# Storing the last of four images in two halves: two PSUM banks, two additions, two stores

## What is computed

```python
def _L3_conv_ref(x, w_qkv, w_out, b_out):
    xf = x.reshape(b, c, n)                          # n = h * w = 256
    qkv = jnp.einsum('oc,bcn->bon', w_qkv, xf)
    qkv = qkv.reshape(b, 3, HEADS, DIM_HEAD, n)
    q, k, v = (qkv[:, 0], qkv[:, 1], qkv[:, 2])
    k = jax.nn.softmax(k, axis=-1)
    context = jnp.einsum('bhdn,bhen->bhde', k, v)
    out = jnp.einsum('bhde,bhdn->bhen', context, q)
    out = out.reshape(b, HEADS * DIM_HEAD, n)
    out = jnp.einsum('oc,bcn->bon', w_out, out) + b_out[None, :, None]
    return out.reshape(b, -1, h, w)
...
x = x + _L3_conv_ref(_gn(x), L3_conv_w_qkv, L3_conv_w_out, L3_conv_b_out)
return x
```

## Time and profile before

| what | us |
|---|---|
| median of 3 timed executions | 65.83 |
| lowest, highest of them | 65.51, 68.95 |
| the profiled execution, its own time | 65.53 |
| its span in the profile | 63.7 |
| granted TensorE clock, mean over the span | 1.0 of full speed |

### The profile page before, as it was taken

The page is one execution under the profiler, slowest core; times in us unless marked ns, Lnnn a source line. Parts: engine busy times, 40 slices in busy tenths (PEclk is TensorE's granted clock), DMA queues, the critical chain, the costliest instruction groups (busy, mean ns, idle before and its releaser), DMA issues. The chain is left out here.

```text
span 63.7 us, 1376 instructions
## 1 busy us (share of the span) xinstructions
PE 58.2 (91%) x362; PEld 47.8 (75%) x362; DVE 48.1 (76%) x218; ACT 36.9 (58%) x113; POOL 34.1 (53%) x98
## 2 busy tenths in 40 slices
PE   2999999999999699799999999999999799999920
PEld 2778748898999488388888688887876579899800
DVE  3848998539899999825579999999999786546350
ACT  5206527997997791780025897537075876796600
POOL 5864986878996364250058997976852142000000
PEclk9999999999999999999999999999999999999999
DMA  0797000000000000000000000000000000001133
GB/s 0 218 241 284 12 0 0 0 0 0 15 5 0 0 0 0 0 5 0 10 0 0 0 0 0 5 0 0 0 0 0 0 0 0 0 10 43 39 116 131
DMA packets 1432, 1.81 MB, mean 28 GB/s; under 512 B 145, under 2 KB 1169, under 8 KB 1425
## 3 DMA queue, kind: packets, MB, share of 16 engines
q1 hardware_dynamic: 1424, 1.73, 8.7%
HBM read 1.20 MB, written 0.52 MB: 27 GB/s over the span
## 5 line engine op out<-in xcount | busy, mean ns | idle before, releaser
L1621 PE MATMUL bank<-x,dw_diag 128*128 128x256 f32 x44 | 11.1, 390 | 0.1
L358 POOL TENSOR_TENSOR gn_rstd<-gn_var_eps,minus_half 128x1 f32<-128x1 f32 x12 | 6.6, 550 | 6.7 <-DVE gn_var_eps L846 6.4
L1621 PEld LDWEIGHTS bank<-x,dw_diag 128*128 128x128 f32 x44 | 7.9, 190 | 1.2 <-DVE x L1115 0.3
L1450 PE MATMUL bank<-warm 128*128 128x256 bf16 x46 | 6.9, 314 | 1.2 <-POOL warm L341 1.2
L1450 PEld LDWEIGHTS bank<-warm 128*128 128x128 bf16 x46 | 5.1, 113 | 2.3 <-POOL warm L341 1.1
L1579 PE MATMUL bank<-vt,probT 128*128 128x128 f32 x32 | 5.1, 281 | 0.0
L1550 PE MATMUL bank<-t,q 128*128 128x256 f32 x16 | 5.0, 392 | 0.0
L679 ACT ACTIVATE h<-dw_sum,kept_scale_bias 128x256 f32<-128x256 f32 x4 | 2.4, 598 | 4.1 <-DVE kept_scale_bias L1182 4.1
L1592 PE MATMUL bank<-signs,conv_blocks 128*128 128x256 bf16 x36 | 4.3, 276 | 0.4 <-ACT signs L638 0.4
L1579 PEld LDWEIGHTS bank<-vt,probT 128*128 128x128 f32 x32 | 4.4, 191 | 0.2
L846 DVE SCALAR_TENSOR_TENSOR gn_var_eps<-gn_group 128x1 f32<-128x1 f32 x16 | 4.3, 271 | 0.1
(11 more groups left out here) (195 smaller groups left out, 164.5 us busy)
## 6 DMA issues: line engine op xcount, KB each, us to landing
out<-x SPq DMA_DIRECT2D x4, 128.0 KB, 1.8
late_params<-in_late SPq DMA_DIRECT2D x1, 404.5 KB, 4.6
early_params<-in_early SPq DMA_DIRECT2D x1, 258.0 KB, 2.7
x<-in_x SPq DMA_DIRECT2D x2, 128.0 KB, 2.5
x<-in_x SPq DMA_DIRECT2D x1, 256.0 KB, 4.1
```

The source lines that it names most:

```text
L358: return nc.gpsimd.tensor_tensor(out_ap, in_ap, minus_half[:, 0:n], ALU.pow)
L1450: nc.tensor.matmul(bank[:, 0:N], warm[:, 0:C], warm[:, :], start=True, stop=True)
L1621: ins = nc.tensor.matmul(dw_ps[b], dw_diag[:, tap, :], xs[2][:, b, dy:dy + H, dx:dx + W], start=(tap == 0), stop=(tap == PE_TAPS[b] - 1))
```

## The change

The output of image 3 is made, added and stored in two halves of 128 columns. On PE, `output(3)` becomes `last_output`, two products of 128 columns, the first into bank 2 and the second into bank 1; it waits beside `q3_ready` and `pj_ready` for the third `e3_ready`, the last reader of what was in bank 1. On DVE, `x4_out(3)` becomes two additions of 128 x 128. On SP, the last store becomes two stores of 64 KB with rows of 512 bytes, each issued when its half has been added; SP then waits for five stores in place of four. Nothing else is changed or moved.

```diff
--- before.py
+++ after.py
@@ -222,6 +222,7 @@
         cx_ps = [banks[i][:, 0:C] for i in (5, 3, 5, 3)]
         pj_ps = [banks[i][:, 0:C] for i in (2, 7, 4, 2)]
         y_ps = [banks[i][:, 0:N] for i in (2, 7, 4, 2)]
+        y_last_ps = [banks[2][:, 0:HALF], banks[1][:, 0:HALF]]
         gn_ps = banks[7]
 
 
@@ -312,10 +313,14 @@
             sp.dma_start(xs[0][:, 1, :], x_v[1]).then_inc(x_in[1], 16)
             sp.dma_start(xs[0][:, 2:B, :], x_v[2:B].rearrange("b c n -> c b n")).then_inc(x_in[2], 16)
             sp.dma_start(lp[:, :], late).then_inc(late_in, 16)
-            for b in range(B):
+            for b in range(B - 1):
                 sp.wait_ge(x4_ready, b + 1)
                 sp.dma_start(out_v[b], xs[4][:, b, :]).then_inc(stored, 16)
-            sp.wait_ge(stored, 16 * B)
+            for half in range(2):
+                side = slice(half * HALF, (half + 1) * HALF)
+                sp.wait_ge(x4_ready, B + half)
+                sp.dma_start(out_v[B - 1][:, side], xs[4][:, B - 1, side]).then_inc(stored, 16)
+            sp.wait_ge(stored, 16 * (B + 1))
 
         @block.gpsimd
         def _(pool):
@@ -1248,6 +1253,15 @@
                 dve.wait_ge(out_bias_ready, b + 1)
                 nc.vector.scalar_tensor_tensor(out=xs[4][:, b, :], in0=y_ps[b],
                                                scalar=out_bias[:, b:b + 1], in1=xs[3][:, b, :],
+                                               op0=ALU.add, op1=ALU.add).then_inc(x4_ready, 1)
+
+            def last_x4_out(half):
+
+                side = slice(half * HALF, (half + 1) * HALF)
+                dve.wait_ge(y3_mm, B + half)
+                dve.wait_ge(out_bias_ready, B)
+                nc.vector.scalar_tensor_tensor(out=xs[4][:, B - 1, side], in0=y_last_ps[half],
+                                               scalar=out_bias[:, B - 1:B], in1=xs[3][:, B - 1, side],
                                                op0=ALU.add, op1=ALU.add).then_inc(x4_ready, 1)
 
             x_arrived(0)
@@ -1441,7 +1455,8 @@
             context_out(3)
             x4_out(1)
             x4_out(2)
-            x4_out(3)
+            last_x4_out(0)
+            last_x4_out(1)
         @block.tensor
         def _(pe):
             def keep_warm(count, bank=warm_ps):
@@ -1714,6 +1729,16 @@
                 pe.wait_ge(pj_ready, b + 1)
                 nc.tensor.matmul(y_ps[b], proj[:, b, :], q3[:, b, :],
                                  start=True, stop=True).then_inc(y3_mm, 1)
+
+            def last_output():
+
+                pe.wait_ge(q3_ready, B)
+                pe.wait_ge(pj_ready, B)
+                pe.wait_ge(e3_ready, 3)
+                for half in range(2):
+                    nc.tensor.matmul(y_last_ps[half], proj[:, B - 1, :],
+                                     q3[:, B - 1, half * HALF:(half + 1) * HALF],
+                                     start=True, stop=True).then_inc(y3_mm, 1)
 
 
             pe.wait_ge(warm_ready, 1)
@@ -1830,7 +1855,7 @@
             project_context(3)
             output(1)
             output(2)
-            output(3)
+            last_output()
 
 
 # ---- launch: one core; the host only lays the inputs out ----
```

## The result

The changed kernel takes 66.17 us (median of 15 executions) against 65.88 us for the kernel before in the same rounds: ratio 1.0054, with a 95% interval of 1.0029 to 1.0079. That is 0.36 us slower (0.2 to 0.5), inside what counts as no change at 2%, but clear of zero. The medians are of all 15 executions, but the ratio leaves out the slow ones, over 1.5% above the fastest of their kernel (67.65 and 116.2 us after, 68.95 before). The forecast was 65.9, with a range of 65.4 to 66.6 and no change as the likeliest.

What follows compares the result with a forecast made beforehand. The prediction took the end to be set by PE's last product, the last addition and the last store, with PE setting the pace. Half 1 landing 0.28 us later on a base of 65.62 gave 65.90 us, range 65.4 to 66.6.

Steps and rivals of the forecast that it cites:

- PE's part: PE's last output: half 0 ready 0.22 us sooner, half 1 no sooner; the added wait costs 0 to 0.11, hidden.
- DVE's part: DVE's last additions: half 0 waits for DVE until 0.21 us after it is ready; the last addition ends 0.08 later.
- SP's part: SP's store queue: half 0's lead of 0.18 us is lost; half 1's store is issued 0.50 later than the last now.
- The landing: Last store, issue to landing: 1.68 us against 1.9; half 1 lands 0.28 later, bounds no change to +0.55.
- The sum: Whole kernel: +0.28 us on a base of 65.62, the mean of three executions, gives 65.90.
- the first two rivals: SP's last stores: Short issue at 65.5 us, chance 0.12, and Rows, not bytes at 66.1, chance 0.24.
- Short issue: SP's last stores: SP is free when half 1 is added, landing 0.14 us before now: 65.5; chance 0.12.
- Rows, not bytes: Last store's transfer: 128 rows of 512 bytes take as long as those of 1024, +0.50 us: 66.1; chance 0.24.
- Code load: Tail: added instructions move a code block's end and an engine stalls for a load, 67.4 us; chance 0.04.

Runs made afterwards that it cites:

- halves of channels: The kernel before, with image 3's store split into two stores of 64 partitions by 1024 bytes, product and addition left whole: ratio 1.0143 (1.009 to 1.0196).

## Why the prediction was right

*PE's part.* The products of the halves start at 60.47, which is 60.33 plus the 0.14 by which this execution runs later, and take 0.61 us together, 0.11 apart. The added wait left no trace: the four follow the ones ahead without a gap. Half 0 was ready at 60.47 + 0.11 + 0.27 = 60.85, and its addition began at 61.07. So PE was covered by 0.22, as the forecast had it (0.21).

*DVE's part.* Forecast: half 0 starts 0.39 after image 2's addition and half 1 another 0.26 later, the last addition ending 0.08 later than before. Measured: 0.40 (61.07 - 60.67), 0.26 (0.60 - 0.34), and 0.08 (1.43 against 1.35).

*SP's part.* Half 0's store starts where the whole one did: 61.61 - 60.24 = 1.37 after the first addition, against 1.38. The second issue was put 0.50 behind the first, and stands 0.50 behind. The runs with one store, with only the store split, and with four stores show that the second issue is the whole cause: without it the loss goes (0.9981), alone it brings the loss (1.0034), and with two more of it the loss grows to 1.021. The tails say the same: +0.01, +0.33 and +1.19, against +0.32 for the change.

*The landing.* The forecast took 1.68 us for the half, from 1.9 less half of the burst's 0.44, and the view says 1.7. In windows of 0.01 us, from the issue's start to SP's next instruction it is 63.35 - 61.48 = 1.87 before and 63.81 - 62.12 = 1.69 after, so 0.18 is saved where 0.22 was forecast. The way there was a little off: the burst shrank from 0.44 to 0.30, by 0.14 and not by half, and 0.04 came from elsewhere. The Trainium skill's page "DMA: Bandwidth & Descriptors", section "Anatomy of one DMA", gives a fit, for transfers issued by GpSimd, from which 0.15 us for 64 KB fewer follows as an estimate, and of the two figures that one comes nearer to the burst. Its fixed cost of 2.0 us doesn't hold for these stores by SP and ACT: in all but the halves of channels they land in 1.6 us (32 KB), 1.7 to 1.8 (64 KB) and 1.7 to 1.9 (128 KB). The forecast also took the spacing of the bursts before, 0.50 us where the issues start 0.43 apart, for a sign of something behind the queue. It is that of the issues' ends: they lie at 60.96, 61.43 and 61.94, and the data starts at 61.46, 61.95 and 62.46, each time 0.50 to 0.52 later.

*The sum.* +0.28 us was forecast, +0.32 is what each of the two tails shows, and +0.36 (0.2 to 0.5) and +0.19 (0.0 to 0.4) what the two timed comparisons do. The time itself, 65.90, was 0.27 under the 66.17 measured, and nearly all of that is the base: I had put it at 65.62, and the kernel before has a median of 65.88 over 15 executions. The range of 65.4 to 66.6 held the times of the first two rivals too, so the time alone says little for the mechanism; the rows and the experiments say it.

*The rivals.* Short issue: no issue of a half or a quarter that follows another on SP by less than 0.05 us is under 0.43 us in any kernel. The same page of the Trainium skill, section "Rules for kernel authors", says that issuing from several engines only saves issue time. The trace agrees: with half 1 issued by ACT the tail is 0.25 us shorter than with both halves on SP. Rows, not bytes: refuted for the transfer, since half the bytes in as many rows takes 0.30 us and not 0.44. Its 66.1 lies near the measured median of 66.17, but only because the base was low. Code load: PE, DVE and SP show no wait in the tail that isn't in the rows above.

## What to carry over

Splitting the last piece of work so that its store can start earlier can pay only if the queue that issues the store is free by then: here the issue of the store ahead ended 0.01 us before the whole one was ready, and the half's lead of 0.18 us was lost entirely. A store over 128 partitions costs its queue 0.33 to 0.46 us, with 32, 64 or 128 KB alike, so n such pieces on one queue end about (n - 1) x 0.5 us later, less what a smaller last transfer saves (0.2 us for halves, 0.3 for quarters here). Before a tail is split, read the issuing queue's rows as one reads an engine's. Giving alternate stores to an engine that is done shortened the profiled tail by 0.05 to 0.13 us, most with whole images; no timed comparison shows that gain over the kernel before.

## What the runs showed of the hardware

The length of an issue goes with how closely it follows the one ahead on its queue, not with its bytes. On SP, over 128 partitions, it is 0.33 to 0.35 us with 0.34 us or more of idle queue ahead of it, 0.38 to 0.39 with 0.09 to 0.13, and 0.43 to 0.46 with about 0.04, for 32, 64 and 128 KB alike. That orders the 0.34, 0.39 and 0.46 of the earlier trace rows, and the 0.38 of the kernel with one store.

The data follows the end of the issue, not its start. Where no other queue was issuing, the first transfer of a store over 128 partitions begins 0.50 to 0.52 us after its issue ends, in the kernels before and after and with quarters. So a longer issue delays the next issue and its own landing.

Two queues issue side by side without a visible delay of the issues: 0.46 and 0.38 us, overlapping, though the data of the second came 0.70 us after its issue's end.

And a store of 64 partitions by 1024 bytes is dearer than one of 128 partitions by 512 bytes, though it has the same bytes and half the rows: 0.53 to 0.59 us to issue and 2.0 to 2.1 us to land, against 0.45 to 0.46 and 1.7.
